# Gate's products from high and low parts inside a scan on Trainium2, and which of three waits the scan operation carries itself

## What is computed

```python
xr, gate = jnp.split(x @ W_in.T, 2, axis=-1)          # 512 -> 1024 and 1024
xc = silu(causal_conv(xr + t_emb))                     # 4 taps, per channel
xn = layernorm(xc) * ln_g + ln_b
Bm, Cm, dt = jnp.split(xn @ W_xproj.T, 3, axis=-1)     # 16 states each
Ad = 1.0 - 0.01 * tanh(dt @ W_dt.T + b_dt) * tanh(A_log)
def step(h, inputs):                                   # 1024 steps, h is [4, 16, 1024]
    h = jnp.clip(h * ad[:, :, None] + bd[:, :, None] * xt[:, None, :], -10.0, 10.0)
    return h, jnp.einsum('bd,bdh->bh', ct, h)
y = ys + D * xn
x = x + y * silu(gate) @ W_out.T
```

## Times and profile before

| | us |
|---|---|
| median of three runs | 2990.14 (2990.12 to 2996.22) |
| the profiled execution | 2992.18 |
| its span, first to last instruction | 2990.4 |
| stage before the scan | 0 to 432 |
| scan's setup | 432 to 474 |
| scan's loop | 474 to 1468 |
| scan's tail | 1468 to 1545 |
| projections, attention, output | 1545 to 2990 |

### The profile page before, as it was taken

One profiled execution on the slowest core, in us unless ns is written; L12 is line 12 of the kernel. 1 busy time (PEld: TensorE's weight loads), 2 busy tenths in 40 slices (PEclk: granted clock), 3 DMA queues, 4 the chain that ended last, 5 costly groups with the idle time before them and its releaser, 6 DMA issues. The chain is left out here.

```text
span 2990.4 us, 52713 instructions
## 1 busy us (share of the span) xinstructions
PE 2813.5 (94%) x19786; PEld 1319.3 (44%) x19786; DVE 2008.8 (67%) x2121; ACT 1114.5 (37%) x1913; POOL 1058.1 (35%) x432
## 2 busy tenths in 40 slices
PE   7999856999999999999879999969999999999999
PEld 3444323454555555555447666643333333333334
DVE  3789865888888888888654344256777677677524
ACT  2677741111111111111121122116666666666620
POOL 0000001134344444434311111016667777777730
PEclk9999958999999999999989999979999999999999
DMA  3245475566667666666634344363334344443364
GB/s 103 100 166 184 172 247 119 126 149 161 161 159 168 153 161 163 157 167 159 174 121 148 126 148 156 118 180 93 83 79 128 90 125 110 96 125 103 97 199 170
DMA packets 246886, 421.86 MB, mean 141 GB/s; under 512 B 45848, under 2 KB 114072, under 8 KB 240360
## 3 DMA queue, kind: packets, MB, share of 16 engines
q1 hardware_dynamic: 164056, 329.92, 37.2%
q10 hardware_dynamic: 82704, 90.32, 13.1%
HBM read 258.88 MB, written 160.98 MB: 140 GB/s over the span
## 5 line engine op out<-in xcount | busy, mean ns | idle before, releaser
L871 DVE CUSTOM_DVE_ANT_0 b_h<-b_h,b_bx,b_bounds_all 128x512 f32<-128x512 f32 x1024 | 825.5, 806 | 171.9 <-PE b_bx L978 110.5
L1503 DVE TENSOR_REDUCE e_half_max<-ef_banks 128x4 f32<-128x2048 f32 x256 | 586.2, 2293 | 236.6 <-PE ef_banks L1456 236.6
L1646 POOL TENSOR_TENSOR e_pair_sum<-e_probs 128x2048 f32<-128x2048 f32 x128 | 585.6, 4575 | 268.3 <-PE ef_banks L1495 215.3
L1615 ACT ACTIVATE e_probs<-ef_banks 128x512 f32<-128x512 f32 x1024 | 555.8, 595 | 313.1 <-PE ef_banks L1470 311.5
L962 POOL TENSOR_TENSOR b_b_weights<-b_bd_all,b_mask_b 128x512 fp32r<-128x512 f32 x64 | 81.5, 1273 | 881.8 <-issue 470.9
L1470 PE MATMUL ef_banks<-e_qs,e_ks 97*128 97x512 f32 x1024 | 383.3, 454 | 3.9 <-DVE e_half_max L1503 3.6
L1028 ACT COPY b_y_stage<-b_y_psum 128x128 f32<-128x128 f32 x256 | 67.8, 265 | 725.8 <-PE b_y_psum L988 725.6
L1470 PEld LDWEIGHTS ef_banks<-e_qs,e_ks 97*128 97x128 f32 x1024 | 155.2, 189 | 332.7 <-ACT e_probs L1615 310.9
L978 PE MATMUL b_bx<-b_x_moving,b_b_weights 24*128 24x512 f32 x1024 | 256.0, 495 | 39.4 <-POOL b_c_weights L964 38.4
L988 PE MATMUL b_y_psum<-b_h,b_c_weights 128*32 128x128 f32 x8224 | 277.8, 276 | 0.5 <-ACT b_y_stage L1028 0.5
L1480 PE MATMUL ef_banks<-e_probs,e_v 128*32 128x512 f32 x2048 | 275.3, 610 | 0.5 <-ACT e_probs L1615 0.4
(11 more groups left out here) (189 smaller groups left out, 3051.9 us busy)
## 6 DMA issues: line engine op xcount, KB each, us to landing
b_x_moving<-xn_parts SPq DMA_DIRECT2D x248, 128.0 KB
e_ks<-qk_parts ACTq DMA_DIRECT2D x42, 512.0 KB, 4.7
e_qs<-qk_parts ACTq DMA_DIRECT2D x84, 256.0 KB, 3.4
xn_full<-a_xn SPq DMA_DIRECT2D x32, 512.0 KB, 3.3
xn_parts<-a_hi SPq DMA_DIRECT2D x64, 256.0 KB, 2.5
xn_parts<-a_lo SPq DMA_DIRECT2D x64, 256.0 KB, 2.5
silu_gate<-b_sg ACTq DMA_DIRECT2D x64, 256.0 KB, 6.0
scan_out<-b_y_stage ACTq DMA_DIRECT2D x256, 64.0 KB, 4.3
```

The source lines that it names most:

```text
L871: return nc.vector._custom_dve(bass.dve_ops.TENSOR_ADD_SAT, **operands)
L1503: nc.vector.tensor_reduce(out=half_max[:, u // UNITS % 2, :, r // NH, r % NH], in_=(banks[:, u % 2 * GROUP:(u % 2 + 1) * GROUP] if u < FIR ...
L1615: nc.scalar.activation(probs[:, g % 4, h, :], p_exp[h % 2], ACT.Exp).then_inc(exps, 1)
L1646: nc.gpsimd.tensor_tensor(out=pair_sum[:, t % 2], in0=probs[:, (2 * t) % 4], in1=probs[:, (2 * t + 1) % 4], op=ALU.add).then_inc(paired, 1)
```

## The change

1. A gate piece becomes three fp32r products, high x high, high x low and low x high. The weights' parts `w_hi` and `w_lo` are made once in the setup. The parts of `x_tile` are made in each iteration: ACT makes `x_hi` of the next iteration's tile after q = 4 and its gate half, waiting for that tile's landing; POOL subtracts for `x_lo` between its two halves; PE's first gate piece waits for `x_split`. SP's load of `x_tile` waits for `x_split` instead of `gate_ready`. The filler product becomes four fp32r products.
2. The gate's weights are loaded by ACT in the stage before, into memory that `x_t1` leaves (`shared`), after the last projection there. The same memory later holds `xn`, `sg_in`, `yg` and `yg_t`.
3. ACT's roots and DVE's inversions move from the tail to the setup; the splits of q, k, v move from the setup to the tail, with the high parts now made by ACT and the low parts by DVE.
4. In `dve_loop` `h_ready` is written first, so that every scan operation carries the wait for the state, and the wait instruction ahead of a pair's first step holds `bx_ready` and `read`.

```diff
@@ pre_phase, ACT, after the last act_round
+                act.wait_ge(projected, START + BATCH * NM)
+                act.dma_start(shared[:], I["w_in_t"][:, INNER:2 * INNER].rearrange("(k p) n -> p k n", p=P)).then_inc(pj.gate_in, 16)
@@ scan_phase, setup, ACT
-                act.dma_start(w_gate[:], I["w_in_t"][:, INNER:2 * INNER].rearrange("(k p) n -> p k n", p=P)).then_inc(weights_in, 16)
                 act.dma_start(x_tile[:], I["x_tiles"][0]).then_inc(tile_in, 16)
                 load_moving(act, 0, 1)
+                pj.roots(act)
+                act.wait_ge(pj.gate_in, START + 16)
+                for half in range(2):
+                    c = slice(half * HALF, (half + 1) * HALF)
+                    nc.scalar.copy(w_hi[:, :, c], w_plain[:, :, c]).then_inc(w_high, 1)
+                act.wait_ge(tile_in, START + 16)
+                nc.scalar.copy(x_hi[:], x_tile[:]).then_inc(x_high, 1)
@@ setup, DVE
-                for n in range(3):
-                    pj.split_mat(dve, n)
+                pj.invert_columns(dve)
+                pj.invert_rows(dve)
+                for half in range(2):
+                    c = slice(half * HALF, (half + 1) * HALF)
+                    dve.wait_ge(w_high, START + half + 1)
+                    nc.vector.tensor_tensor(out=w_lo[:, :, c], in0=w_plain[:, :, c], in1=w_hi[:, :, c].bitcast(f32), op=ALU.subtract)
+                dve.wait_ge(x_high, START + 1)
+                nc.vector.tensor_tensor(out=x_lo[:], in0=x_tile[:], in1=x_hi[:].bitcast(f32), op=ALU.subtract).then_inc(x_split, 1)
@@ piece_of
-                    pe.wait_ge(weights_in, START + 16)
-                    pe.wait_ge(tile_in, START + it * 16 + 16)
+                    pe.wait_ge(x_split, START + it + 1)
...
-                mm = nc.tensor.matmul(gate[:], x_tile[:, k, :], w_gate[:, k, half * HALF:(half + 1) * HALF], start=(k == 0), stop=(k == NK - 1))
+                c = slice(half * HALF, (half + 1) * HALF)
+                for part, (x_part, w_part) in enumerate(((x_hi, w_hi), (x_hi, w_lo), (x_lo, w_hi))):
+                    mm = nc.tensor.matmul(gate[:], x_part[:, k, :], w_part[:, k, c], start=(k == 0 and part == 0), stop=(k == NK - 1 and part == 2))
...
-                nc.tensor.matmul(p_out[:], w_gate[:, m % NK, 0:P], w_gate[:, m % NK, HALF:2 * HALF], start=True, stop=True)
+                for part in (w_hi, w_hi, w_lo, w_lo):
+                    nc.tensor.matmul(p_out[:], part[:, m % NK, 0:P], part[:, m % NK, HALF:2 * HALF], start=True, stop=True)
@@ new
+        def split_high(act, it):
+            act.wait_ge(tile_in, START + it * 16 + 16)
+            act.wait_ge(gate_ready, START + it * 2)
+            nc.scalar.copy(x_hi[:], x_tile[:]).then_inc(x_high, 1)
+        def split_low(pool, it):
+            pool.wait_ge(x_high, START + it + 1)
+            nc.gpsimd.tensor_tensor(out=x_lo[:], in0=x_tile[:], in1=x_hi[:].bitcast(f32), op=ALU.subtract).then_inc(x_split, 1)
@@ sp_loop
-                    sp.wait_ge(gate_ready, START + it * 2)
+                    sp.wait_ge(x_split, START + it)
@@ pool_loop
+                if i == 1 and split:
+                    split_low(pool, it)
@@ dve_loop
-                dve.wait_ge(bx_ready, START + it * PAIRS + (v + 1))
-                dve.wait_ge(read, START + it * PAIRS + (v + BEFORE - 1))
                 for u in (2 * v, 2 * v + 1):
                     t = it * STEPS + u
                     dve.wait_ge(h_ready, START + it * STEPS + u)
+                    if u % 2 == 0:
+                        dve.wait_ge(bx_ready, START + it * PAIRS + (v + 1))
+                        dve.wait_ge(read, START + it * PAIRS + (v + BEFORE - 1))
@@ act_loop
                 if q == 4:
                     take_gate(act, it, 1)
+                    if more:
+                        split_high(act, it + 1)
@@ tail, ACT
-                pj.roots(act)
                 for j in range(first - 1, last):
-                    take_turned(act, j, 0)
-                    take_turned(act, j, 1)
+                    for g in range(2):
+                        take_turned(act, j, g)
+                        n = 2 * (j - first + 1) + g
+                        if n < 3:
+                            pj.split_high(act, n)
@@ tail, DVE
-                pj.invert_columns(dve)
                 mix(dve, nc.vector, first)
                 add_x(dve, nc.vector, first - 1)
+                for n in range(3):
+                    pj.split_low(dve, n)
                 mix(dve, nc.vector, first + 1)
-                pj.invert_rows(dve)
```

More of the change, by code:

```diff
@@ L36, with __init__ @@
     MATS = "qkvwu"
-    def __init__(self, nc, I, X1, WDC, stack):
+    def __init__(self, nc, I, X1, WDC, stack, early):
         self.nc, self.I, self.X1, self.WDC, self.stack = nc, I, X1, WDC, stack
@@ L43, in __init__ @@
         self.consts = sem("consts")
+        self.gate_in = sem("gate_in")
         self.u_in = sem("u_in")
@@ L80, in __init__ @@
         self.rows = sb("rows", [BATCH, 3, MODEL]); self.qk = sb("qk", [P, 2 * NK * BATCH]); self.qk_col = sb("qk_col", [P, NK * BATCH])
-        self.plain = ExitStack()
-        self.w = {j: self.plain.enter_context(nc.sbuf_tensor("d_w_" + j, [P, NK, MODEL], f32, side="right")) for j in "qkv"}
+        self.w = {j: early.enter_context(nc.sbuf_tensor("d_w_" + j, [P, NK, MODEL], f32)) for j in "qkv"}
     def sb(self, n, s, d=f32):
@@ L157, in sum_squares, with split_high, split_low @@
         mm.then_inc(self.sums, 1)
-    def split_mat(self, dve, n):
+    def split_high(self, act, n):
         j = self.MATS[n]
-        self.nc.vector.tensor_copy(out=self.w_hi[j][:], in_=self.whole(j)).then_inc(self.split, 1)
+        self.nc.scalar.copy(self.w_hi[j][:], self.whole(j)).then_inc(self.split, 1)
+    def split_low(self, dve, n):
+        j = self.MATS[n]
         dve.wait_ge(self.split, START + n + 1)
@@ L236, in sem @@
             return sems[-1]
-        w_in = sb("w_in", [P, NK, INNER]); x_t = [sb(f"x_t{i}", [P, NK, SEQ]) for i in range(2)]
+        w_in = sb("w_in", [P, NK, INNER]); x_t = [sb("x_t0", [P, NK, SEQ]), shared]
         cols = sb("cols", [P, sum(COLS.values())])
@@ L762, in scan_phase @@
         w_out = sb("w_out", [P, NM, MODEL], f32); d_row = sb("d_row", [P, INNER], f32); ident = sb("ident", [P, P], f32)
-        xn = sb("xn", [P, INNER], f32); y = sb("y", [P, INNER], f32); sg_in = sb("sg_in", [P, INNER], f32); yg = sb("yg", [P, INNER], f32)
-        yg_t = sb("yg_t", [P, NM, P], f32); x = sb("x", [P, MODEL], f32); o = sb("o", [P, MODEL], f32); x1 = sb("x1", [P, MODEL], f32)
+        y = sb("y", [P, INNER], f32)
+        w_plain = shared; xn, sg_in, yg = (shared[:, i, :] for i in range(3)); yg_t = shared[:, 3, :].rearrange("p (m t) -> p m t", t=P)
+        x = sb("x", [P, MODEL], f32); o = sb("o", [P, MODEL], f32); x1 = sb("x1", [P, MODEL], f32)
         p_turn = pb("p_turn", [P, HALF], f32); p_out = pb("p_out", [P, MODEL], f32)
-        pj.parts()
         loop = ExitStack()
@@ L781, in scan_phase @@
         zeros = sb("zeros", [P, HALF], bf16)
-        w_gate = sb("w_gate", [128, NK, INNER], f32); x_tile = sb("x_tile", [128, NK, 128], f32); sg = sb("sg", [128, 2, HALF], f32)
+        w_hi = sb("w_hi", [P, NK, INNER], f32r); w_lo = sb("w_lo", [P, NK, INNER], f32r)
+        x_tile = sb("x_tile", [P, NK, P], f32); x_hi = sb("x_hi", [P, NK, P], f32r); x_lo = sb("x_lo", [P, NK, P], f32r); sg = sb("sg", [128, 2, HALF], f32)
         gate = pb("gate", [128, HALF], f32)
@@ L952, in sp_loop, with pool_loop @@
                     load_x(sp, j + (-1), *before)
-        def pool_loop(pool, it, j, out=False):
+        def pool_loop(pool, it, j, out=False, split=True):
             for i in range(2):
+                if i == 1 and split:
+                    split_low(pool, it)
                 t0 = it * STEPS + i * T
@@ L1059, in _ @@
             def _(pool):
-                with pool.Fori(0, LAG) as it:
+                pool_loop(pool, 0, None, split=False)
+                with pool.Fori(1, LAG) as it:
                     pool_loop(pool, it, None)
@@ L1084, in _ @@
                     act_loop(act, it, None)
-                with act.Fori(0, TILES - OUT_LAG) as j:
+                with act.Fori(0, TILES - OUT_LAG - 1) as j:
                     act_loop(act, j + OUT_LAG, j)
+                act_loop(act, LOOPS - 1, TILES - OUT_LAG - 1, more=False)
                 for i in range(2):
@@ L1091, in scan_phase @@
         loop.close()
+        pj.parts()
         pj.rest()
@@ L1757, in build @@
     with ExitStack() as kept:
-        pj = Projections(nc, I, X1, WDC, kept)
-        pre_semaphores = pre_phase(nc, I, pj, Xp, Xn, Bp, Pd, Iv, Cm)
-        scan_phase(nc, I, Xp, Xn, Bp, Pd, Iv, Cm, Y, SG, X1, pj, pre_semaphores)
+        early = ExitStack()
+        shared = early.enter_context(nc.sbuf_tensor("shared", [P, NK, INNER], f32))
+        pj = Projections(nc, I, X1, WDC, kept, early)
+        pre_semaphores = pre_phase(nc, I, pj, shared, Xp, Xn, Bp, Pd, Iv, Cm)
```

(2 more changed lines are left out.)

19 lines of the change are left out of this document (9 added, 10 removed).

## The result

The changed kernel took 3011.4 us (median of 4 runs, 3007.4 to 3014.8) against 2991.6 for the kernel before on the same chip: a ratio of 1.0063, 95% interval 1.0045 to 1.0082. It is slower by 0.6%, some 20 us, where I had forecast no change.

A forecast was written before the change was run, and what follows sets the result against it. PE was taken to bound the loop, transfers the setup, a chain of mixes the tail. Terms: weights 0, setup -10, loop +13, tail -0.4, wait order 0: +2.6 on 2990.14 gives 2992.7 us, range 2977 to 3008.

The forecast's parts named there:

- The three products: Gate blocks in the loop: each saves 0.31 us (3.47 long), 1.25 per iteration, giving 29.81 if PE stayed unhindered.
- The new wait: ACT's wait for the next `x_tile` delays its copy; PE stands 1.57 us before block 14's readouts, period 31.40 against 31.06.
- the rival with the tile in time: Loop: `x_tile` lands under 5.1 us after its issue, PE does not stand, time 2943 us; chance 0.13.
- The clock: PE's granted clock in the steady loop, read as 1.00 before the change; the sum had no term for it.
- The first tile: Loop's start: tile 1 lands 10.0 us after issue instead of 6.7, PE already waited about 1: +2 us once.
- filled iterations: First five iterations: the larger filler adds 0.16 us in each of four blocks, two already covered: +1.5 us in all.
- The setup: Before the scan: constants land earlier without 2 MB of gate weights beside them; -10 us, bounds nothing and -11.8.
- the setup stays, slower: Rival: twelve small copies set the setup's end, constants land only 3 us earlier, total 2999.7 us; chance 0.20.
- Early weights: ACT issues gate weights near 371 us, where transfers move 12 GB/s: zero, at most 0.4 us.
- order of waits: DVE's gaps between pairs fall from 0.17 to 0.03 us, 29.1 to 27 per iteration; zero while PE leads.
- The tail: After the scan: splits move in, inversion moves out, a table load is added; -0.4 us, bounds -3 and +2.
- the mix behind the splits: Tail: DVE's three low parts take 6.9 us and end at 1497.2, delaying the mix that started at 1495.28 by 1.9.

The follow-up runs named there:

- the first experiment: The changed kernel with SP issuing the next `x_tile` ahead of the eight `x_moving` transfers instead of behind them: 2992.0 us, ratio 0.9988.
- The filled stretch: The changed kernel with six more fp32r products (1.4 us) per iteration where PE stood before block 14's readouts: 3001.8 us, ratio 1.0023.
- the kernel before with two casts: The kernel before, its gate one fp32 product, with ACT's wait for the next `x_tile` and two casts into unread buffers added: 3066.6 us, ratio 1.0238.
- the split kernel: The changed kernel with `x_tile` issued half an iteration ahead, plus the setup's twelve small constant copies split over two queues: 2944.5 us, ratio 0.9838.

## Why the prediction was wrong

**The three products: right.** Two copies of ACT with a gate block between them, in the kernel after:

```profile
902.70 0.27 ACT L1056 COPY b_y_stage<-b_y_psum 128x128 f32<-128x128 f32 x1 [3.52 <-PE b_y_psum L1015]
906.16 0.27 ACT L1056 COPY b_y_stage<-b_y_psum 128x128 f32<-128x128 f32 x1 [3.19 <-PE b_y_psum L1015]
```

They are 3.46 us apart, forecast 3.47. Unhindered the loop takes 29.7 an iteration, forecast 29.81.

**The new wait: right in kind, place and size.** Forecast were an idle of 1.57 us before block 14's readouts released by ACT's copy, a cast that waits for the tile, and a period of 31.40. Measured were 39.3 us in 26 iterations (1.51), and 31.26 in iterations without a fall. The landing, taken as 6.7, is

```profile
DMA to landing us min/median/max: 6.3/6.8/7.3
```

It is also why the rival with the tile in time did not hold. The estimate of 2.6 us that I had worked out from the Trainium skill's DMA: Bandwidth & Descriptors, section Anatomy of one DMA, comes from a fit that the page gives for transfers issued by GpSimd. The traces agree with it where nothing is ahead of the tile on SP's queue (2.7/2.9/3.9 us in the first experiment), and not where eight others are (6.3/6.8/7.3).

**The clock: the step that failed.** The sum took the clock of the earlier trace rows, 1.00, for granted in a loop that would no longer keep PE busy. It has eight falls of 1.55 us in the steady iterations and one of 1.54 in the second. A tenth lies within the first tile's long stall and reaches past it: the readouts take 1.93 us (below) for 1.08, and from there to the next block's readouts it is 5.40 us, where the third and fourth iterations take 3.45. That one costs 1.95. Together they are +16 us. The filled stretch shows the cause, and the kernel before with two casts shows it again with other products. The prediction priced an idle of 1.57 us at 1.57. At that price the profiled execution would have taken 2999 us (3014.8 - 16), inside the range.

**The first tile: mis-sized.** Forecast was +2. It landed 12.8 us after its issue where it had taken 10.0, and PE stood for 6.74 us:

```profile
506.36 1.93 PE L1015 MATMUL b_y_psum<-b_h,b_c_weights 128*32 128x128 f32 x32 [6.74 <-ACT b_y_stage L1056]
```

Without its fall the first iteration is 36.3 us, 5.8 more than the third and fourth; in the kernel before it was 1.4 more. So the first tile costs 4.4 us, not 2, and the 2.4 above the forecast are about the 2.8 by which it landed later than before. The second tile also came late (a stall of 2.56 us), and the other filled iterations were shorter than forecast: together the first five are, without falls, 7.3 us longer than before, where the sum had 5.2. The steady iterations gave that back: without the cost of the falls they are longer by 0.25 each, not by 0.34.

**The setup: mis-sized, -4.1 instead of -10.** DVE's chain ended at 456.3, forecast 456.4. The constants did not: 464.31, against 468.25. Over all eleven profiles of kernels with part 3 the scan starts 36.2 to 38.8 us after the setup's first memset, over three without it 41.2 to 43.0. The mean gain is 5 us. The rival "the setup stays, slower" decided by a landing after 460 us, and it did; its 2999.7 is the nearest of my numbers to the result, in part by luck, since it has nothing of the clock that makes most of the miss. I had read DVE's 23.76 us of waiting as the price of 2 MB, while the row named the small copies at the end of the queue.

**Early weights and order of waits: right. The tail: right in its sum, in part by luck.** From the last scan operation to the first product of the projections the tail gave -0.5 (forecast -0.4), but this stretch lies between 73.0 and 77.3 us over the eleven profiles with part 3, so -0.5 cannot be told from nothing. Its parts are of another size than I had them: the mix behind the splits comes 1.3 us later (forecast 1.9), the next one 4.4 us earlier (forecast 1.7), and what follows gives that back. The table load is where it was expected:

```profile
1554.00 1.28 ACT L219 ACT_TABLE_LOAD   x1
```

The sum of the misses: +16 (falls), +6 (setup), -1 (the rest of the loop), -1 (behind the scan) make the 20 us between 2.6 and 22.6.

## What to carry to other kernels

Where an engine waits for a transfer, ask what else is queued behind that wait; issuing the transfer half an iteration ahead was worth 62 us here, and the same transfer moved only a few places forward made the ones it passed late. A stall of a TensorE that has been busy without a gap can cost more than its length: here it did from 1.2 us on, in some iterations and not in others. Count it at its length plus the products at half clock behind it, and see by the granted clock of short windows whether these are there. When several transfers end a setup, the row that says which landed last is the one to price.

## What the runs showed of the hardware

In the steady loop the granted clock fell to its lower level (1.2 GHz) behind idle stretches of 1.2 to 2.4 us on a TensorE that was otherwise busy: behind none of the 52 stretches of at most 1.4 us in two of the kernels, behind 5, 7, 8, 14 and 16 of 26 in those with longer ones. In the first iterations a stretch of 2.56 us had a fall and one of 2.7 us (the split kernel) had none. A fall cost 1.55 us with fp32r products and 1.61 with fp32, and 1.4 us of other products in the stretch prevented all that had stood in the steady iterations. A transfer of 256 KB on SP's queue landed 2.9 us after its issue with nothing ahead of it and 6.8 us behind eight others. The constants, twelve small transfers last, had landed 30 to 33 us after the setup's start in every arrangement tried with the gate's weights out of the way, while DVE was ready up to 10 us before them.
